# PE takes the later of two overlapping stages first; the attention's row root on ScalarE for 15 of 16 batches

## What is computed

```python
x = x + _L0_xattn_ref(_layernorm(x), ctx_2048, ctx_2048)            # part A
x = x + _L0_ffn_ref(_layernorm(x), L0_ffn_w1, L0_ffn_w2)            # FFN b, inner 1024, gelu twice
x = x + _L1_xattn_ref(_layernorm(x), ctx_2048, Wq, Wk, Wv, Wo, ...) # attention C, 16 heads, 4 KV heads, RoPE
x = x + _L1_ffn_ref(_layernorm(x), w1, w2, w3)                      # FFN d, inner 704, silu(gate) * up
def _layernorm(x, axis=-1, eps=1e-05):
    m, v = mean(x), var(x)
    return (x - m) / sqrt(v + eps)
```

## Time and profile before

| | us |
|---|---|
| runs: median (lowest to highest, 3 runs) | 853.86 (850.46 to 861.3) |
| profiled execution, its own time | 858.67 |
| its span, first to last instruction | 856.5 |
| busy: DVE, PE, ACT, POOL | 725.7, 696.1, 645.8, 486.2 |
| share of the span | 85%, 81%, 75%, 57% |
| mean granted clock of TensorE | 0.951 |

### The profile page before, as it was taken

How to read it: one execution, slowest core, us unless ns; L and a number is a source line. 1 busy time by engine, 2 the same in 40 slices (tenths; PEclk the granted TensorE clock), 3 DMA queues, 4 the chain that set the end, 5 groups by cost and what they waited for, 6 DMA issues and landing times. The chain is left out here.

```text
span 856.5 us, 16817 instructions
## 1 busy us (share of the span) xinstructions
PE 696.1 (81%) x4627; PEld 416.2 (49%) x4627; DVE 725.7 (85%) x1826; ACT 645.8 (75%) x2140; POOL 486.2 (57%) x668
## 2 busy tenths in 40 slices
PE   0185888888737677999999999999999999855876
PEld 0152333333313344666666666666666666533443
DVE  7667598888579968999999999999999999885796
ACT  0656577777449948999999999999999999863452
POOL 1500021121236788888788878888888888621453
PEclk9996699999969989999999999999999999989997
DMA  8402444444304327876978688778778788651235
GB/s 279 166 1 68 141 124 148 142 136 135 87 22 93 90 63 142 142 136 126 149 138 129 132 151 139 139 129 148 139 138 135 131 151 143 118 97 27 56 96 129
DMA packets 321999, 103.90 MB, mean 121 GB/s; under 512 B 286933, under 2 KB 321143, under 8 KB 321655
## 3 DMA queue, kind: packets, MB, share of 16 engines
q1 hardware_dynamic: 321910, 102.89, 58.2%
HBM read 22.10 MB, written 6.29 MB: 33 GB/s over the span
## 5 line engine op out<-in xcount | busy, mean ns | idle before, releaser
L1327 ACT ACTIVATE psum<-psum,arena 128x256 f32<-128x256 f32 x256 | 136.8, 535 | 29.1 <-DVE arena L1439 29.1
L1395 DVE SCALAR_TENSOR_TENSOR arena<-psum,arena 128x256 f16<-128x256 f32 x256 | 110.9, 474 | 1.1 <-ACT arena L1344 1.1
L1528 PE MATMUL psum<-arena 128*128 128x512 f16 x384 | 94.4, 382 | 16.5 <-DVE arena L1422 16.3
L1344 ACT ACTIVATE arena<-psum,arena 128x256 f16<-128x256 f32 x256 | 100.5, 475 | 8.7 <-issue 4.5
L1490 PE MATMUL psum<-wq_t,arena 128*128 128x512 f16 x384 | 95.8, 387 | 4.5 <-ACT arena L1358 3.9
L1543 PE MATMUL psum<-wo_t,arena 128*128 128x256 f16 x768 | 96.4, 276 | 3.3 <-DVE arena L1422 3.3
L1515 PE MATMUL psum<-arena 128*128 128x256 f16 x768 | 94.3, 273 | 1.6 <-DMA arena<-arena 0.8
L1281 POOL TENSOR_TENSOR arena<-arena 128x512 f32<-128x512 f32 x64 | 81.2, 1268 | 21.6 <-DVE arena L1414 21.5
L1543 PEld LDWEIGHTS psum<-wo_t,arena 128*128 128x128 f16 x768 | 76.0, 99 | 26.9 <-DVE arena L1422 3.7
L1312 POOL TENSOR_TENSOR arena<-arena 128x512 f16<-128x512 f32 x64 | 74.1, 1158 | 20.0 <-DVE arena L1439 19.9
L346 POOL TENSOR_TENSOR arena<-arena 128x256 f32<-128x256 f32 x16 | 12.0, 747 | 126.1 <-DVE arena L425 126.1
(11 more groups left out here) (188 smaller groups left out, 1704.0 us busy)
## 6 DMA issues: line engine op xcount, KB each, us to landing
arena<-split_scratch SPq DMA_DIRECT2D x96, 64.0 KB, 2.7
arena<-arena SPq DMA_TRANSPOSE x272, 3.3
arena<-in_x SPq DMA_DIRECT2D x32, 128.0 KB, 2.3
split_scratch<-arena SPq DMA_DIRECT2D x32, 128.0 KB, 1.8
arena<-in_L_ffn_w SPq DMA_DIRECT2D x2, 1024.0 KB, 7.2
x_rows<-in_L_xattn_Wq SPq DMA_DIRECT2D x1, 2048.0 KB, 14.3
ctx_t<-in_L_xattn_Wo SPq DMA_DIRECT2D x1, 2048.0 KB, 12.4
arena<-in_ctx SPq DMA_DIRECT2D x16, 128.0 KB, 2.1
```

The source lines that it names most:

```text
L1327: last = eng.activation(s_banks(u)[:, h, :], s_banks(u)[:, h, :], ACT.Exp, bias=bias[:, u % 2, h:h + 1], scale=r_q(u)[:, h:h + 1], accum_o ...
L1344: hi = eng.activation(p_hl[:, u % 2, 0, h, :], s_banks(u)[:, h, :], ACT.Copy, scale=share[:, u % 2, h:h + 1])
L1395: last = eng.scalar_tensor_tensor(p_hl[:, u % 2, 1, h, :], s_banks(u)[:, h, :], share[:, u % 2, h:h + 1], p_hl[:, u % 2, 0, h, :], ALU.mul ...
L1528: mm = eng.matmul(A_BANK, v[:, u % V_SLOTS, x, k, :], p_t[:, u % 2, w, :, k, :], start=(n == 0), stop=(n == 5))
```

## The change

```diff
-    eps = c.local("eps_c", [P, 1])
+    eps = c.local("eps_c", [P, 2])
...
     def pool(eng):
-        eng.memset(eps[:, :], 1e-6 * W_SCALE * W_SCALE).then_inc(S["eps"], 1)
+        eng.memset(eps[:, 0:1], LN_EPS).then_inc(S["eps"], 1)
+        eng.memset(eps[:, 1:2], 1e-6 * W_SCALE * W_SCALE).then_inc(S["eps"], 1)
...
         for s in range(STEPS):
-            b = batch(s, ROWS)
-            if b is not None:
+            if batch(s, ROWS) == 0:
+                b = 0
                 eng.wait_ge(S["stats"], 2 * (b + 1))
                 eng.tensor_scalar(var[:, :], mv[:, 1:2], 1.0, LN_EPS, ALU.mult, ALU.add).then_inc(S["rstd"], 1)
                 eng.wait_ge(S["rstd"], 2 * b + 1)
-                wait(eng, S["y"], b)
                 eng.tensor_tensor(rstd[:, :], var[:, :], c.minus_half[:, 0:1], ALU.pow).then_inc(S["rstd"], 1)
...
     def scalar(eng):
-        eng.wait_ge(S["eps"], 1)
+        eng.wait_ge(S["eps"], 2)
...
-                eng.activation(log_ms[:, :], sums[:, u % 2, :], ACT.Ln, scale=1.0 / HEAD_DIM, bias=eps[:, :])\
+                eng.activation(log_ms[:, :], sums[:, u % 2, :], ACT.Ln, scale=1.0 / HEAD_DIM, bias=eps[:, 1:2])\
                    .then_inc(S["r"], 1)
+            b = batch(s, ROWS)
+            if b:
+                eng.wait_ge(S["stats"], 2 * (b + 1))
+                wait(eng, S["rstd"], 2 * b)
+                eng.activation(var[:, :], mv[:, 1:2], ACT.Ln, bias=eps[:, 0:1]).then_inc(S["rstd"], 1)
+                eng.wait_ge(S["rstd"], 2 * b + 1)
+                wait(eng, S["y"], b)
+                eng.activation(rstd[:, :], var[:, :], ACT.Exp, scale=-0.5).then_inc(S["rstd"], 1)
             score = unit(s, SCORE)
...
         def in_step(n, eng):
-            running = [(stage[n](eng), start) for stage, start in stages]
+            running = [(stage[n](eng), start) for stage, start in (stages if n < 4 else stages[::-1])]
             for step in range(D_START + BATCHES + 16):
```

## The result

| | before | after |
|---|---|---|
| first set of runs: median, lowest to highest | 857.58, 850.46 to 861.85 (4) | 829.61, 828.21 to 841.32 (4) |
| ratio in that set | | 0.968, 95% 0.958 to 0.977 |
| second set: median | 853.64 (19) | 829.99 (4), ratio 0.975, 95% 0.971 to 0.980 |
| third set: median | 850.91 (11) | 833.25 (6), ratio 0.974, 95% 0.968 to 0.980 |
| span of the first profile | 856.5 | 827.2 |

The ratios leave out runs in a slower state, here the one of 841.32 us, and are not the quotients of the medians beside them, which would be 0.967, 0.972 and 0.979.

The account below looks back on a forecast made before the run. VectorE and TensorE were taken to bound the attention alone, and a serial chain through VectorE, PE and ScalarE its end. Terms -15.4, 0, -6.5, +0.4 sum to -21.5 of 858.67; the same share off 853.86 gives 832.5 us, range 826 to 843.

Parts of the forecast that it names:

- the serial chain at the end: 763 to 802 us, second FFN starting as attention runs out: VectorE's gate product idles for ScalarE's Silu, 15.4 us in four times.
- the stretched instruction in the root's step: One attention step of four: GpSimd's row root delays L1294, so VectorE's L1439 takes 0.69 in place of 0.19 us.
- part 1: PE's order at the end: FFN's wide product taken before the attention's matmuls removes all four idles, -15.4 us, bounds 7.2 to 15.7.
- part 3: Row root moved from GpSimd to ScalarE: 0.50 us gained in each of 13 attention steps, -6.5 us, bounds 0 to -6.6.
- Part 2: PE's order at the beginning, steps 20 to 24: first FFN's down product goes later but stays covered, cost 0, bounds 0 to +1.0.
- between 0 and 0.15 late: Root's step on ScalarE: how late the first exponential starts behind the added Ln and Exp, in us.
- The start-up's +0.4: Moved roots of batches 1 and 2, where ScalarE has no idle ahead: about 0.2 us each, bounds 0 to 0.8.
- 1 (ScalarE takes the 0.50 back): Root's step: Ln, its wait and Exp make ScalarE last, so only the end pays; 838.9 us, chance 0.13.
- 2 (the product at the low clock): At the end, the wide product in front runs at low clock and hands it on; 836.5 us, chance 0.12.
- the ring: At the end: VectorE's gate product, PE's attention matmuls and wide product, ScalarE's Silu, gate product again; 7.16 us for one step.
- 3 (only the product leaves the ring): At the end, ScalarE's square, waiting for L926, stands ahead of the next Silu; 840.7 us, chance 0.09.
- 4 (more table loads): Attention: moved Ln and Exp make ScalarE reload tables, so slower; 865.9 us, chance 0.04 shared with any other loss.

## Why the prediction was right, and where it was not
**What bounds the kernel.** Shown: removing the serial chain at the end and the stretched instruction in the root's step each moved the time by itself, by 15.5 us for 15.4 of waits and by 5.9 us for 6.6 of stretch.

**The sum.** -21.5 forecast and -21.5 measured is closer than the parts allow, and partly luck: part 1 brought 0.35 more than its term, three stretches without an edit 0.2 more together, and part 3 0.6 less. The stretches of the three profiles of after differ by up to 0.5 as well.

**Part 1.** The forecast was -15.4, of at most 15.7; it measured -15.75, and -15.5 alone. Against the other two kernels with the old order at the end (57.4 and 56.7) it would be 15.25 and 14.5. Each step of the working can be read in the new timeline. L926 of tiles 0 to 4 starts 26.2, 29.7, 34.0, 38.4 and 42.2 us after unit 63's rotation product, before 30.5, 37.6, 45.6, 53.8 and 57.9: 4.3, 7.9, 11.6, 15.4, 15.7 earlier, so each of the four idles went (4.14, 3.58, 3.58, 4.08). Next late is VectorE itself, as said. I had Silu of tile 0 ready 0.8 us before L926 and it was 0.7. The tightest was not tile 3 with 0.2 but tile 1 with 0.5 (Silu ends at 759.64, L926 starts at 760.14); tile 3 had 0.6. PE has work of both stages in steps 86 to 89, four steps and not five, which is why there were four idles.

**Part 2.** 0, and measured so. What hides the later down product is as predicted: L872's waits are the same to 0.1 us. The reserve was smaller than I had it: tile 11's L971 ends at 299.47 and its L872 starts at 301.68, 2.2 us in place of 3.1. The projections ahead of it took longer, 1.49 and 1.47 (L1510) where it was 1.04 and 0.82, with a granted clock of 0.59 from 293.2 to 299.5 us after 4.4 us without a matmul. VectorE covered that too.

**Part 3.** -6.5 forecast, -5.9 measured. The mechanism was right: the stretch went, all of it (18.1 to 11.4 us in the group's sum). The term that was off is "so between 0 and 0.15 late", which I then took as 0; it is 0.07 in a step, 0.9 in all, shown by leaving the pair out. The prices behind it were right. The record of L1379 (Ln) is 0.35 long and not 0.20, but it starts 0.20 after L1373, which is still running, and ends 0.18 after it (416.84 against 416.66). The Exp waits for the semaphore of the Ln, starts 0.03 after it and ends at 417.07: the pair ends 0.41 after L1373, as the 0.40 of the forecast. Less the 0.09 by which L1328 overlaps the Exp, the working gave 0.05 late, and 0.05 to 0.07 it is. Only the step from there to 0 was wrong. The start-up's +0.4 came out at +0.4 in the first profile and at 0.15 and 0.2 in the other two, and at 0.3 to 0.6 against the kernel without the pair; since unedited stretches differ by as much, only its size is supported.

**The rivals.** 1 (ScalarE takes the 0.50 back) fell: 0.07. 2 (the product at the low clock) fell the other way round: the granted clock from 749 to 773 us is 1.00, the level of 2.4 GHz, where the earlier trace rows has 0.87, and L1537 takes 1.46 in place of 2.72. The new order fills the idle time ahead of it: 3.86 us in one piece became 0.61 and 1.31 with matmuls between. What I had not seen is that the low clock was part of the ring before. There the way from L1528 to Silu took 7.52 us for tile 0, at a granted clock of 0.60, and 4.59 and 4.60 for tiles 1 and 2, at 1.00; the one from L1543 to Silu took 4.99 for tile 3, at 0.66, and 3.3 for tile 1. By these differences, an estimate, some 4.6 of the 15.4 us of idle were TensorE partly at the lower level of its clock, after gaps of 3.86 and 3.32 us (the gaps of 2.61 and 3.41 us ahead of tiles 1 and 2 did not bring it). No run separates this share from the order; in the new order both are gone, and L926 waits for nobody. 3 (only the product leaves the ring) fell with the idles. 4 (more table loads) fell: between the attention's load at 293.93 and Silu's at 753.81 there is none. That agrees with what the Trainium skill (ScalarE: Activation LUTs, Table sets: the hidden batching unit) says, that ln and exp lie in one set. A change of tables costs 1.32 us here, from the end of L791 at 753.79 to the first Silu at 755.11, and not the 2.66 of the estimate beside rival 4.

**The 7.8 us too many.** The first part of the program, up to the table load, has no edit in any of these kernels. It ends at 240 to 252 us, and does so with kernels of either order and either root. The kernel after has 240.10, 240.29 and 250.04 in three profiles. What goes with it is TensorE's granted clock. The stretch from 60 to 240 us in the first profiles of before and after:
```profile
60.00:240.00 180.00, 144.19 (x891) 61.51 (x889) 133.97 (x330) 121.53 (x193) 28.07 (x37) 0.87 0.39 117
```
```profile
60.00:240.00 180.00, 136.86 (x895) 59.74 (x893) 141.59 (x370) 120.71 (x192) 31.34 (x43) 0.90 0.39 118
```
TensorE is busy 7.3 us longer in the first row, for four matmuls less. Over all 12 profiles:

| granted clock, 60 to 240 us | table load at | VectorE's L412 waits for PE's L518 |
|---|---|---|
| 0.90 (3 profiles) | 239.86, 240.10, 240.29 | 18.8 to 19.3 |
| 0.88, 0.89 (4) | 239.82, 240.51, 242.83, 243.11 | 18.1 to 21.0 |
| 0.86, 0.87 (5) | 247.90, 249.91, 250.04, 251.65, 252.29 | 25.6 to 30.0 |

L518 is a product of part A, L412 its reader. The wait in the first profiles of before and after (us in total, times, longest):
```profile
DVE arena L412 <- PE psum L518: 25.6, 15, 4.6
```
```profile
DVE arena L412 <- PE psum L518: 18.8, 15, 4.5
```
Of the 7.8 us between the two, 6.8 stand in this one wait: VectorE waited for a slower TensorE. The first pair of profiles thus shows 7.8 us that the change did not make, and the medians of the first set a part of it: before has 857.58 there and 853.64 and 850.91 in the larger sets. Against these 19 and 11 runs of before the ratio is 0.975 and 0.974, which is what the sum gave. So the forecast was right by its sum as well, and nearer than the first result shows.

What stays open is why the clock is granted so differently in the first part; that it is the cause is argued from these rows, since no run sets it. Not tried either: whether SP's earlier transposes for tiles 2 and 3 are needed for the gain at the end; no run holds them back.

## What to carry to other kernels
Where two stages share in-order engine queues, look at the few steps in which they overlap and ask, engine by engine, whose operand is ready first: PE stood behind a matmul whose operand came 3.4 us later (765.82 against 762.41) than that of the one queued behind it, and turning its order alone was worth 15.5 us. A tiny instruction that takes several times its usual duration in one step of four can be stretched by a neighbour on another engine, and the group view's mean gives it away (283 against 178 ns); moving the neighbour shows whether it is so. An instruction that is stretched in every step, as L1469, is not seen in the mean: there the shortest one is to be compared. In a chain with gaps on TensorE, read the granted clock of each piece: here a lower clock made up an estimated 4.6 of 15.4 us. Before a difference of profiles is explained, subtract the stretch that no edit touches.

## What had not been expected of the hardware
- The same instructions took 240 to 252 us up to the Gelu table load, with a mean granted clock of 0.90 to 0.86 from 60 to 240 us; from there on the same kernel repeated within 0.5 us (587.10, 586.81, 587.26).
- Not only the small L1439 is stretched by a GpSimd operation of two tensors. L1469, a tensor-scalar operation of 256 columns, takes 0.41 with no GpSimd instruction beside it (the first one with the root late on GpSimd, at 289.53 us), 0.70 in the steady steps before and after, where L1315 (L1316 after) starts 0.17 ahead, and 0.89 when it starts with L1315 (423.75 and 423.76). In the last two cases it ends 0.15 after L1315. So it is still stretched in the kernel after, by 0.3 us in each root's step.
- The duration of an activation in the profile need not be its price. Ln of a single column takes 354 ns in its group's mean here and 202 in part A (L370, 16 times), where ScalarE mostly stood idle ahead of it. Here it is issued while L1373 still runs, and ends only 0.18 after it. The second of a dependent pair starts when the first is over (416.49 + 0.35 to 416.87).
